# Moving the output stores of a two-stage graph kernel from the SyncE queue to the ScalarE queue

## The reference

```python
summed = jax.ops.segment_sum(x[src], dst, num_segments=n)
aggr = summed / jnp.maximum(cnt, 1.0)[:, None]
h = aggr @ W_l.T + b_l + x @ W_r.T
mu = jnp.mean(h, axis=0)
var = jnp.mean(jnp.square(h - mu), axis=0)
h_norm = (h - mu) * jax.lax.rsqrt(var + EPS) * gamma + beta
x = _layernorm(x + jax.nn.relu(h_norm), axis=-1)
```

## Time and profile before

| | |
|---|---|
| median of 3 runs | 2672.82 us (2671.72 to 2673.6) |
| the profiled execution, time | 2667.74 us |
| its span | 2666.0 us |
| stage two, from the first scale | 1940 us to the end, 726 us |
| bytes moved in the whole span | 753 MB, mean 283 GB/s |
| ACT busy, whole span | 1452.2 us (54%) |
| POOL busy, whole span | 1437.0 us (54%) |
| DVE busy, whole span | 1955.3 us (73%) |

### The profile page before, as it was taken

How to read it: one execution, slowest core, us unless ns; L and a number is a source line. 1 busy time by engine, 2 the same in 40 slices (tenths; PEclk the granted TensorE clock), 3 DMA queues, 4 the chain that set the end, 5 groups by cost and what they waited for, 6 DMA issues and landing times.

```text
span 2666.0 us, 29300 instructions
## 1 busy us (share of the span) xinstructions
PE 1760.2 (66%) x9404; PEld 1420.5 (53%) x9404; DVE 1955.3 (73%) x3302; ACT 1452.2 (54%) x2766; POOL 1437.0 (54%) x834
## 2 busy tenths in 40 slices
PE   5599999999999999999999999996300000000000
PEld 4477777888887777888877777884200000000000
DVE  7746777888877777878877777885588666666665
ACT  3234444555454444445554444542369788778888
POOL 5344454555555554455555555454186666666663
PEclk9799999999999999999999999997755555555555
DMA  4267678888887777888878777887589999999996
GB/s 148 88 197 226 222 253 254 257 259 262 265 253 252 229 248 249 253 265 261 265 247 270 254 246 229 249 270 253 164 324 425 425 426 426 426 426 426 426 421 269
DMA packets 126473, 753.47 MB, mean 283 GB/s; under 512 B 22007, under 2 KB 22007, under 8 KB 66412
## 3 DMA queue, kind: packets, MB, share of 16 engines
q1 hardware_dynamic: 72652, 619.04, 60.4%
q0 software_dynamic: 53664, 132.51, 19.9%
HBM read 515.92 MB, written 246.22 MB: 286 GB/s over the span
## 4 chain that ended last, share of the span: by engine, by line
PE 49%; DMA 24%; DVE 11%; ACT 7%; issue 6%; POOL 2%; SPq 0%; DVEq 0%; POOLq 0%; ACTq 0%
DMA out<-hx 12%; PE pd L492 10%; PE pd L494 10%; PE pd L493 10%; DMA hx<-h_scratch 6%; PE pz L597 4%; PE pz L598 4%; PE pz L599 4%; DMA xf<-x,gi 4%; ACT hx L813 3%; ACT hx L823 3%; DVE x_lo L969 2%; PE px L591 2%; POOL hx L1313 2%; DMA hs<-h_scratch 1%
## 5 line engine op out<-in xcount | busy, mean ns | idle before, releaser
L1293 POOL DMA_INDIRECT h_scratch<-zz,si x156 | 302.8, 1941 | 684.5 <-ACT zz L736 469.8
L492 PE MATMUL pd<-wc_hi,x_hi 128*128 128x512 f32 x1564 | 638.2, 408 | 41.3 <-POOL x_lo L1220 24.5
L494 PE MATMUL pd<-wc_hi,x_lo 128*128 128x512 f32 x1564 | 617.9, 395 | 0.0
L493 PE MATMUL pd<-wc_lo,x_hi 128*128 128x512 f32 x1564 | 616.3, 394 | 0.0
L1313 POOL TENSOR_TENSOR hx<-hx,scale_b 128x2560 f32<-128x2560 f32 (+1 forms) x79 | 438.8, 5556 | 268.1 <-DMA hx<-h_scratch 218.8
L691 ACT ACTIVATE h_out<-pd 128x512 f32<-128x512 f32 x391 | 233.0, 596 | 397.8 <-PE pd L494 397.8
L813 ACT ACTIVATE hx<-hx,nm 128x512 f32<-128x512 f32 x391 | 276.6, 708 | 142.8 <-POOL nm L1319 142.8
L492 PEld LDWEIGHTS pd<-wc_hi,x_hi 128*128 128x128 f32 x1564 | 297.8, 190 | 103.0 <-POOL x_lo L1220 24.5
L1245 POOL DMA_INDIRECT xn<-x,gi x156 | 308.2, 1976 | 47.7 <-issue 44.6
L494 PEld LDWEIGHTS pd<-wc_hi,x_lo 128*128 128x128 f32 x1564 | 297.0, 190 | 65.7
L493 PEld LDWEIGHTS pd<-wc_lo,x_hi 128*128 128x128 f32 x1564 | 298.1, 191 | 56.2
(11 more groups left out here) (216 smaller groups left out, 2930.0 us busy)
## 6 DMA issues: line engine op xcount, KB each, us to landing
raw<-xT_whole SPq DMA_DIRECT2D x78, 1280.0 KB, 7.7
h_scratch<-h_out SPq DMA_DIRECT2D x78, 1280.0 KB, 10.6
hs<-h_scratch SPq DMA_DIRECT2D x78, 1280.0 KB, 13.0
hx<-h_scratch SPq DMA_DIRECT2D x78, 1280.0 KB, 15.4
hx<-x SPq DMA_DIRECT2D x78, 1280.0 KB, 20.6
out<-hx SPq DMA_DIRECT2D x78, 1280.0 KB, 18.0
xn<-x,gi POOLq DMA_INDIRECT x156, 8.1
xf<-x,gi POOLq DMA_INDIRECT x156, 7.2
```

The lines of the kernel that those rows point to most:

```text
L492: pe.matmul(pd[i][0:n, :], hi, wc["hi"][:, kc, :], start=kc == 0, stop=False)
L493: pe.matmul(pd[i][0:n, :], hi, wc["lo"][:, kc, :], start=False, stop=False)
L494: last = pe.matmul(pd[i][0:n, :], lo, wc["hi"][:, kc, :], start=False, stop=kc == KC - 1)
L1293: pool.indirect_dma_start(out=h_dram[:, :], out_offset=by, in_=zz[:, h, :], in_offset=None, bounds_check=N + 2 * P - 1, oob_is_err=True, c ...
```

## The change

The store of a group is issued by ACT, in ACT's own DMA queue, directly behind the normalisation that fills its buffer. SP keeps the loads. SP now waits for `s_oa` itself before it loads x into a buffer that ACT has read, and its loop ends with the last load. ACT, too, waits for `s_oa` before the store: a DMA reads what ACT's own instructions have written, and the wait makes sure that they have ended.

```diff
-            def store2(k):
-                i = k % NB2
-                sp.wait_ge(s_oa, TG * k + tiles_in(k))
-                sp.dma_start(group_of(out, k), part_of(hb[i], k)).then_inc(s_os[i], 16)
-
-            for k in range(G + 1):
-                store2(k)
+            for k in range(G + 2 - NB2):
                 if k + NB2 <= G:
+                    sp.wait_ge(s_oa, TG * k + tiles_in(k))
                     load2_x(k + NB2)
-                if k >= 1 and k - 1 + NB2 <= G:
+                if k >= 1:
                     load2_h(k - 1 + NB2)
...
+            def store2(k):
+                act.wait_ge(s_oa, TG * k + tiles_in(k))
+                act.dma_start(group_of(out, k), part_of(hb[k % NB2], k)).then_inc(s_os[k % NB2], 16)
+
             for k in range(G + 2):
                 if k <= G:
                     squares2(k)
                 if k >= 1:
                     normalise(k - 1)
+                if 1 <= k <= G:
+                    store2(k - 1)
+            store2(G)
```

## The result

The changed kernel takes 2678.46 us (median of 20 runs), the kernel before 2671.44 us (20 runs). The ratio is 1.0029, 95% interval 1.0021 to 1.0037: some 7.7 us slower. The forecast was slower by 11.9 us; on the three runs shown then that was 2684.7 us.

What follows compares the result with a forecast made beforehand. The prediction took DMA transfers, full in the middle of stage two, to bound the kernel. Its terms, 8.3 + 3.0 + 0.6 = 11.9 us, added to the median of 2672.82, gave 2684.7 us, range 2677 to 2692.

Steps and rivals of the forecast that it cites:

- What bounds it: Middle of stage two: the transfers are full at 425 GB/s, no compute engine is; a group costs 9.35 us.
- Who goes first: Loads of h in stage two: stores on their own queue overtake, 2.65 transfers more before the same h, +8.3 us.
- A store alone: Store landing in stage two: with both queues served in turn, about 7.6 us instead of 18.0.
- ACT's issues: ACT's last groups: five stores between squares 74 and normalise 78 cost 0.6 us each, +3.0 us; hidden in the middle.
- a wait 0.6 us shorter per group: Sign in the profile after: ACT's waits in the middle as before, less 0.6 us.
- Start: Start of stage two, queue not yet full: ACT reaches store 1 later by one issue, +0.6 us (0.3 to 0.9).
- The rate: Transfer rate of two queues in stage two: no change, with 0.6% of 650 us, about 4 us, as bound either side.
- the order of issue was not kept: Rival, chance 0.14: engines take transfers as issued, a store still needs 18 us; 2679.5 us.
- the better packing: Rival, chance 0.19: a second queue fills stalls, the cycle falls from 9.35 to 9.22 us, 1.4%, 9.1 us; 2675.6, no change.
- the rise of the rate: Rival, chance 0.11: loads and stores overlap in two queues; decides from 2.6% on, 437 GB/s; at 3%, 2665 us.
- the rate did not fall: Denies a rival, chance 0.06: changing between read and write with each packet costs 2% or more, 13 us on top, 2698.
- the five gaps on ACT: Sign in the profile after: ACT ends with five gaps of 0.6 us.

## Why the prediction was right

- **What bounds it.** Right. The middle is bound by transfers, and the chain of waits was mostly queueing. The store's time fell by 7.7 us and SP's wait for stores by 409 us with no gain. One reading was loose: ACT is without idle time from squares 74 on, not from scale 76; 3.64 us of idle time stand between the two.
- **Who goes first, +8.3 us.** Right in mechanism, too large: 4.8 us at scale 76, and these hold the start. The step that was mis-sized is "when h of group j lands, exactly stores 0 to j-8 stand before it". For h 76 that makes 69 stores, and with the loads up to it 206 transfers, 270.0 MB; one queue had moved 273.37 MB by then, 2.6 transfers more. The two queues, too, were ahead of the order of issue, in loads: 137 transfers, 179.6 MB, stand there up to h 76, and 181.11 MB had been moved, 1.2 transfers more. The difference of 1.4 is missing from the forecast. The stores after the change were well counted: 72.0 against my 71.65. So the net lead is 1.6 transfers, not 2.65.
- **Why more had moved.** SP's queue after the change, from the first store to the end of the span:

```profile
q1 hardware_dynamic: 20064, 181.22, 61.5%
```

So when h 76 counted as landed, 181.11 of 181.22 MB were through, nearly all of h 77 and 78 behind it. A transfer lands with its last piece, and what stands behind it goes on meanwhile. Which of the DMA engines holds that piece, no view shows, nor why the last loads come late in both kernels: scale 75 and 76 start 10.2 and 11.1 us after the scale ahead of them before, 11.3 and 11.1 after, where 9.3 is the mean. Up to scale 74, ahead of this end, the two queues had moved 268.3 MB in 632.5 us and the one 265.6 MB in 628.7: a lead of 2.05 transfers, 6.4 us, of which a higher rate (424.1 instead of 422.4 GB/s) gave 2.5 back; 3.8 us were measured there.
- **A store alone.** 7.6 us was forecast for its landing, 10.3 measured. Half rate against a full queue was too hopeful; it didn't matter much, since only what is done before the last h counts.
- **ACT's issues, +3.0 us.** Each cycle of ACT in the last groups went from 7.38 us (the mean of three) to 7.90: 0.52 each, 5 x 0.52 = 2.6. Behind scale 76 the kernel loses 2.2, since the last store's own way is 0.4 shorter. In the middle they were hidden in ACT's waits, as forecast. But the sign named for it, a wait 0.6 us shorter per group, didn't come: 102.4 / 56 = 1.83 us instead of 1.87. The profile doesn't count an issue as busy, so this wait holds the issue.
- **Start, +0.6 us.** Store 1 comes 7.96 us behind store 0 instead of 7.39: 0.57. What it is worth at the end isn't shown; where ACT only spent time, store 1 came 0.44 later and scale 76 only 0.1.
- **The rate.** Nearly no change: 420.6 and 420.7 GB/s from the first store to h 76. In the middle it rose a little, from 425 to 427 in the window, in both profiles of each kernel, and from 170.4 to 170.8 MB in the 400 us from 2100. That is 0.2 to 0.4%, 1.5 to 2.5 us of 650, within the bound of 0.6%; the slower end took it back.
- **The sum.** 11.9 forecast; 7.0 in the profiles, 7.7 by the ratio. The direction and the mechanism held; at scale 76 the forecast's 8.9 us (8.3 and 0.6) were 4.8, behind it 3.0 were 2.2. The rivals: the order of issue was not kept (10.3 us, not 18), the better packing and the rise of the rate came to 0.4% at most, where 1.4% and 2.6% were needed, and the rate did not fall.
- **What would show it.** h from issue to landing in "about 33 us" was 31.9; the five gaps on ACT are there; scale 76, forecast near 2628, started at 2629.81, which with stage one's 4.7 us taken off is 2625.1.

## What to carry to other kernels

When transfers bound a stage and its end is bound by something else, what counts is which transfers go before the last load, not how soon each one is issued or lands. Stores moved to a queue of their own overtake loads and use up bandwidth that would have been free at the end; look for the transfers that can wait until the last loads are through. And count the time of a stage from its own first event, so that another stage's scatter doesn't pass for an effect.

## What the runs showed of the hardware

- A transfer of 16 rows of 4 bytes to HBM, once per 9.8 us, cost 0.49 us of the full queue and took the middle from 425 to 399 GB/s; with 2048 bytes per row (and the rows further apart) the middle was back at 425. The Trainium skill ("DMA: Bandwidth & Descriptors", "Specifications") says that below 512 bytes the engine reads, changes and writes back. The fall agrees with that; no run shows the mechanism.
- Two hardware queues, one with stores and one with loads, moved about as much as one with both: 427 and 425 GB/s in the middle, 420.7 and 420.6 up to h 76.
- A queue's bytes run ahead of its landings: when h 76 counted as landed, 2.6 transfers issued behind it had moved in the one queue, 1.2 in the load queue of two.
- A DMA issue on ACT whose wait is already met runs beside activations. One that has to wait for the activation ahead of it takes ACT 0.52 us.
